# Denominator sums of cross-attention: four steps to a tile in 24 quarters of the second sequence, and one bank for the last turn

## The chip, the cores and the metric

The kernel runs on one core of one Trainium2 chip. The metric is the time on the device, in microseconds (us), of one execution. Names of engines: TensorE (PE) multiplies matrices, VectorE (DVE) and ScalarE (ACT) read and write its result banks, GpSimd (POOL) adds between tiles and issues some of the DMAs, SyncE (SP) issues the others.

## The reference, cut to what matters

A decoder layer over two sequences of 1024 tokens with 512 numbers each: a linear attention, a cross-attention to 2048 context rows, and a mixture of eight experts, each followed by a layer norm. The change lies in the cross-attention:

```python
q = (x1 @ wq.T)...; k = (x2 @ wk.T)...; v = (x2 @ wv.T)...   # 16 heads of 32
dots = jnp.einsum('bhnd,bhmd->bhnm', q, k) * SCALE
attn = jax.nn.softmax(dots, axis=-1)
out = jnp.einsum('bhnm,bhmd->bhnd', attn, v)
```

The softmax divides by the sum of exponentials over the 2048 context rows: the denominators. Numerators and denominators are summed apart, and the division comes last.

## The kernel before, in words

The attention runs in 16 **turns**. A turn takes one group of four heads of one sequence and one half (512) of its queries. Turns 0 to 7 are the first sequence, 8 to 11 the first half of the second sequence's queries, 12 to 15 the second half; 15 is LAST. A turn has 16 **steps**, one for each 128 context rows. A step has four scores (one matmul of 98x128 by 98x512 for each head, L1409), four exponentials on ScalarE (L2165) that write a tile `probs` of 128 x 4 x 512, and the numerators (L1420, eight records).

The loop goes by **blocks** of two steps, eight to a turn. The scores of the following block alternate with matmuls for the maxima (L1390) of a turn about one and a half ahead; VectorE takes each maximum (L1752, 64 to a turn, up to the fourth block of turn 14). Then come one unit of side work (rows after the attention, router), due shifts, the numerators of both steps, due divisions and inversions, and the visits for the denominators. Every engine follows the same plan in its own order; a wait stands in front of an instruction and holds all that is behind it on that engine.

**Denominators.** The two tiles of a block are added to one: GpSimd in four instructions (`add_head`, L2287) or, from the middle of turn 14, VectorE in one (`add_pair`, L1766). Four steps are a **quarter**. A *plain* quarter sends each pair's sum to TensorE; a quarter *by fours* adds its two sums into one by an accumulating DMA on GpSimd's queue (`add_four`, L2291), issued one block after the second pair. `by_fours` decides: all of turns 0 to 7 but the last quarter, and what is in LATER_FOURS. TensorE sums a tile over its partitions by eight matmul records with ones (L1442), into a bank taken from the ring `next_s_bank`; that is a **visit**, and a visit takes all tiles of a turn that are due. A pair is due one block after its addition, a quarter by fours four blocks after its second pair, or three if it is in LAST_BEFORE_PLAIN. VectorE turns the bank into `den_t` (L1773), after the visit before it has been added; GpSimd (in turn 15 VectorE: L1782, L1785) adds one column of each block of `den_t` to `den_s`. There is one `den_t` and one `den_s`. After the last visit of a turn VectorE inverts (L1793, L1794) and GpSimd divides (L2327); the first addition of a turn waits for the inversion of the turn before.

**Banks.** Eight. Bank 6 holds the numerators. Scores go round banks 0, 1, 2; maxima, shifts, side work and denominators round 4, 5, 3, 7. From the fifth block of turn 14 on there are no maxima and all share one ring of seven: 0 to 5 and 7 (SPARE). Whoever takes a bank waits until its holder before has been emptied: a denominator bank by the transpose, a score bank by the exponential.

**The end.** The last visit of turn 15 has three tiles: the sum of steps 12 and 13, and steps 14 and 15 as they are. The numerators of these two stand behind it in TensorE's order, then the inversion and division by quarters of the queries, the output rows, the router and the experts.

Lines of the excerpt: `by_fours`, `den` and `add_den` in the tables of signals, `denominators`, `add_denominators`, the loop over turns, `denominators_of`, `turn_den`, `add_den`, `invert`.

## Time and profile before

| | us |
|---|---|
| median of 3 runs | 1871.95 |
| lowest, highest | 1870.49, 1872.1 |
| the profiled execution | 1867.24 |
| its span (first to last instruction) | 1865.3 |
| attention loop, turns 0 to 15 | about 484 to 1363 of the span |
| busy: TensorE, VectorE, ScalarE, GpSimd | 1838.5, 1260.0, 878.8, 849.6 |

Busy time of TensorE is modelled from overlapping matmuls, so that a busy TensorE need not be at its peak; where it loses time is to be seen in the order of time. A turn ends where ScalarE copies its numerators out of bank 6 (L2173): turn 7 at 876.0, turn 8 at 943.8, turn 9 at 1001.3, turn 10 at 1070.2, turn 11 at 1129.4, turn 12 at 1188.5, turn 13 at 1254.6, turn 14 at 1304.5, turn 15 at 1362.9. The granted clock of TensorE is 0.997 of full speed over the span.

### The profile page before, as it was taken

To read this page: it belongs to the slowest core of one execution; us is meant where nothing else is said; L and a number is where in the kernel's file an instruction comes from. 1 tells how busy PE (TensorE), PEld (TensorE's weight loads), DVE (VectorE), ACT (ScalarE), POOL (GpSimd) and SP (SyncE) were. 2 spreads that over 40 slices of the span, in tenths; PEclk is the share of its full clock that TensorE was granted. 3 is DMA by queue.
4 is the path that set the end of the run, shared out by engine and by line. 5 is a ranking of instruction groups with operands and counts; after the bars stand their busy time and mean duration, and the time that the engine had idled before them with its cause. 6 is when DMAs were issued, how large, how long until landed. Compare 5 with 4: busy or idle time off the path is not lost.

```text
span 1865.3 us, 27888 instructions
## 1 busy us (share of the span) xinstructions
PE 1838.5 (99%) x10488; PEld 1290.2 (69%) x10488; DVE 1260.0 (68%) x2352; ACT 878.8 (47%) x1587; POOL 849.6 (46%) x822
## 2 busy tenths in 40 slices
PE   9999999999999999999999999999989999999998
PEld 8786687778655555555555554554469998899986
DVE  6675574278787888888798699778554444344457
ACT  4322323221666666666465465557624443344433
POOL 4002201000598999998677677676122223222232
PEclk9999999999999999999999999999999999999999
DMA  8003525684767686758445443451244454534544
GB/s 289 24 1 118 194 96 180 200 241 145 169 141 167 136 201 130 173 120 178 106 131 121 101 115 88 112 114 65 78 156 122 131 141 108 144 90 133 142 113 153
DMA packets 124502, 250.19 MB, mean 134 GB/s; under 512 B 11312, under 2 KB 29504, under 8 KB 119680
## 3 DMA queue, kind: packets, MB, share of 16 engines
q1 hardware_dynamic: 109696, 187.56, 34.2%
q0 software_dynamic: 14672, 60.85, 15.9%
q8 instruction: 83, 1.36, 0.3%
q14 instruction: 51, 0.42, 0.1%
HBM read 148.46 MB, written 62.42 MB: 113 GB/s over the span
## 4 chain that ended last, share of the span: by engine, by line
PE 87%; DVE 9%; DMA 2%; issue 1%; POOL 1%; ACT 0%; SPq 0%; DVEq 0%; POOLq 0%; ACTq 0%
PE banks L1221 36%; PE banks L1534 12%; PE banks L1409 11%; PE banks L1420 11%; PE banks L1390 10%; DVE max L1752 5%; PE banks L1442 4%; PE banks L1227 2%; DVE den_t L1773 1%; PE banks L1321 1%; DMA k_stack<-k_parts 0%; DMA k_half<-in_xwk_t 0%; POOL x_nat L2298 0%; DVE hot_row L1937 0%; DVE probs L1766 0%
## 5 line engine op out<-in xcount | busy, mean ns | idle before, releaser
L2287 POOL TENSOR_TENSOR probs<-probs,probs 128x512 f32<-128x512 f32 x464 | 584.4, 1304 | 192.2 <-PE banks L1420 191.4
L1752 DVE TENSOR_REDUCE max<-banks 128x1 f32<-128x512 f32 x1024 | 625.7, 678 | 37.9 <-PE banks L1390 37.5
L2165 ACT ACTIVATE probs<-banks 128x512 f32<-128x512 f32 x1024 | 517.6, 626 | 283.8 <-PE banks L1409 283.2
L1409 PE MATMUL banks<-q_stack,k_stack 98*128 98x512 f32 x1024 | 403.0, 406 | 1.1 <-DVE den_t L1773 1.0
L1390 PE MATMUL banks<-k_stack,q_stack 98*128 98x512 f32 x1024 | 399.2, 398 | 1.9 <-DVE den_t L1773 1.3
L1409 PEld LDWEIGHTS banks<-q_stack,k_stack 98*128 98x128 f32 x1024 | 190.9, 187 | 151.3 <-issue 100.6
L1420 PE MATMUL banks<-probs,v_grp 128*32 128x512 f32 x2048 | 249.7, 600 | 0.0
L1390 PEld LDWEIGHTS banks<-k_stack,q_stack 98*128 98x128 f32 x1024 | 192.4, 188 | 48.1 <-DVE max L1752 13.1
L2347 POOL DMA_INDIRECT y_rows<-eo,tok x35 | 69.8, 1994 | 173.3 <-DVE eo L1992 118.9
L1420 PEld LDWEIGHTS banks<-probs,v_grp 128*32 128x32 f32 x2048 | 60.1, 109 | 117.9 <-issue 111.6
L1979 DVE TENSOR_TENSOR hid_lo<-hid,hid_hi 128x640 fp32r<-128x640 f32 x64 | 52.7, 824 | 126.4 <-ACT hid_hi L2234 126.4
L1221 PE MATMUL banks<-w_hi,hid_hi 128*128 128x512 f32 x320 | 128.7, 402 | 0.0
L2298 POOL TENSOR_TENSOR x_nat<-x_nat,bxo_row 128x512 f32<-128x512 f32 x16 | 21.2, 1359 | 232.4 <-PE banks L1227 232.4
L1221 PE MATMUL banks<-w_hi,hid_lo 128*128 128x512 f32 x320 | 126.3, 395 | 0.0
L1221 PE MATMUL banks<-w_lo,hid_hi 128*128 128x512 f32 x320 | 125.9, 393 | 0.0
L1534 PE MATMUL banks<-xe_hi,w_hi 128*128 128x320 f32 x512 | 118.8, 309 | 0.0
L1534 PE MATMUL banks<-xe_hi,w_lo 128*128 128x320 f32 x512 | 118.7, 309 | 0.0
L1534 PE MATMUL banks<-xe_lo,w_hi 128*128 128x320 f32 x512 | 118.6, 309 | 0.0
L2229 ACT ACTIVATE hid<-banks,b1c 128x640 f32<-128x640 f32 x64 | 50.8, 793 | 139.8 <-PE banks L1534 139.8
L1773 DVE STREAM_TRANSPOSE den_t<-banks 128x512 f32<-128x512 f32 x84 | 59.9, 713 | 80.0 <-PE banks L1442 75.9
L2338 POOL DMA_INDIRECT xg<-x_rows,tok x40 | 39.1, 977 | 156.7 <-PE banks L1227 127.9
L1442 PE MATMUL banks<-probs,ones 128*32 128x512 f32 x744 | 98.1, 593 | 3.6 <-DVE probs L1766 2.0
(274 smaller groups left out, 2795.6 us busy)
## 6 DMA issues: line engine op xcount, KB each, us to landing
k_stack<-k_parts SPq DMA_DIRECT2D x144, 256.0 KB, 5.3
probs<-probs POOLq DMA_DIRECT2D x36, 1024.0 KB, 9.9
w_raw<-in_L_ffn_w SPq DMA_DIRECT2D x16, 2048.0 KB, 9.5
q_stack<-q_parts SPq DMA_DIRECT2D x48, 256.0 KB
v_grp<-v_rows SPq DMA_DIRECT2D x48, 256.0 KB, 3.6
raw<-in_ctx_t SPq DMA_DIRECT2D x8, 1024.0 KB, 6.4
k_parts<-out_hi SPq DMA_DIRECT2D x32, 256.0 KB, 2.6
k_parts<-out_lo SPq DMA_DIRECT2D x32, 256.0 KB, 3.1
```

The costliest lines, as they stand in the source:

```text
L1221: done = nc.tensor.matmul(out, lhsT, rhs, start=start and n == 0, stop=stop and n == len(operands) - 1)
L1390: nc.tensor.matmul(out, queries_of(t)[:, j, tile_of(k)], keys_of(t)[0:STK + SHIFT, j, mc * HALF:(mc + 1) * HALF], start=True, stop=True) \
L1409: nc.tensor.matmul(out, keys_of(t)[0:STK + SHIFT, j, tile_of(s)], queries_of(t)[:, j, :], start=True, stop=True).then_inc(scored.sem, 1)
L1420: done = nc.tensor.matmul(bank(NUM)[j * DH:(j + 1) * DH, :], v_grp[:, s, j * DH:(j + 1) * DH], probs_of(t, s)[:, j, :], start=s == 0, stop ...
L1442: done = nc.tensor.matmul(out[j * DH:(j + 1) * DH, :], ones[:, 0:DH], tile[:, j, :], start=n == 0, stop=n == len(tiles) - 1)
L1534: done = nc.tensor.matmul(both[:, h, 0:HC], w, x[:, h * HC:(h + 1) * HC], start=n == 0, stop=n == len(terms) - 1)
L1752: V.reduce_max(max4[:, tiles_of(t), :, :][:, k, j, mc:mc + 1], bank(bank_of["max", t, mc, k, j]), AX.X) \
L1773: V.transpose(den_t[:, :], bank(bank_of["den", t, s])).then_inc(den_turned.sem, 1)
L1979: V.tensor_tensor(hid_lo[:, f, :], hid[f % 2][:, :], hid_hi[:, f, :].bitcast(F32), ALU.subtract) \
L2165: S.activation(probs_of(t, s)[:, j, :], bank(bank_of["score", t, s, j]), ACT.Exp, scale=SCALE) \
L2287: G.tensor_tensor(a[:, j, :], a[:, j, :], b[:, j, :], ALU.add).then_inc(pair_added.sem, 1)
L2347: G.indirect_dma_start(out=y_rows, in_=eo[turn % EO][:, :], in_offset=None, compute_op=ALU.add, out_offset=bass.IndirectOffsetOnAxis(ap=to ...
```

## The change

1. LATER_FOURS, five quarters before, holds 24: all quarters of turns 8 to 13 but the last of turn 11, and the first of turn 14. (11, 2) joins (7, 2) in LAST_BEFORE_PLAIN.
2. In turn 15 all visits sum into one bank, SPARE, which is taken at the first visit. `start` is set only there and `stop` only at the last. VectorE turns the bank once, after the last visit, and takes the reciprocals from `den_t` itself; `add_den` is gone for this turn on both engines, and with it the signal last_den_added.
3. From the fifth block of turn 14 the common ring has six banks, 0 to 5, and denominators of turn 15 take none of them.

```diff
--- before.py
+++ after.py
@@ -56,9 +56,9 @@
 TILES_Y = 2
 FOUR = 4
 
-LAST_BEFORE_PLAIN = {(2 * NG - 1, 2)}
-
-LATER_FOURS = {(8, 0), (8, 1), (10, 1), (13, 0), (13, 1)}
+LAST_BEFORE_PLAIN = {(2 * NG - 1, 2), (3 * NG - 1, 2)}
+
+LATER_FOURS = {(t, q) for t in range(2 * NG, 4 * NG - 2) for q in range(4)} - {(3 * NG - 1, 3)} | {(4 * NG - 2, 0)}
 PARTS = 3
 PIECES_Y = B * NT // TILES_Y
 HALF_Y = B * NT // 2
@@ -365,7 +365,7 @@
         ones_in, xwo_in, y_in = signals("ones_in", 2, 64), signal("xwo_in", 4 * 16), signals("y_in", NH, 16)
         parts_in = signal("parts_in", 16)
         max_scored, max_taken = signal("max_scored"), signal("max_taken")
-        top_taken, inverted, den_turned, last_den_added = signals_on("tops_inverses", 4)
+        top_taken, inverted, den_turned = signals_on("tops_inverses", 3)
         top_hi, shift_copied = signals_on("shift_parts", 2)
         shift_turned = signal("shift_turned")
         scored, exp_done = signal("scored"), signal("exp_done")
@@ -453,8 +453,8 @@
             "add_pair": lambda t, s: (last_pair_added,),
             "add_head": lambda t, s, j: (pair_added,),
             "add_four": lambda t, s: (fours_added[four_of(t, s)],),
-            "den": lambda t, s: (den_summed, den_turned),
-            "add_den": lambda t, s: (last_den_added if t == LAST else den_added,),
+            "den": lambda t, s: (den_summed, den_turned) if t < LAST or s == MT - 1 else (den_summed,),
+            "add_den": lambda t, s: (den_added,),
             "copy_num_tile": lambda t, k: (num_copied,),
             "invert": lambda t, k: (inverted,),
             "divide": lambda t, k: (divided,),
@@ -852,15 +852,22 @@
                 den_steps[visit] = steps
                 den_visit.update(((t, s), visit) for s in steps)
                 den_begun.setdefault(t, visit)
-                do("den", *visit, ring=next_s_bank)
-                summed.append(visit)
+                if t < LAST:
+                    do("den", *visit, ring=next_s_bank)
+                    summed.append(visit)
+                    continue
+                if den_begun[t] == visit:
+                    take_bank(("den", t, MT - 1), SPARE)
+                do("den", *visit)
+                if steps[-1] == MT - 1:
+                    divisions.extend((t, k) for k in BY_VECTOR + BY_TENSOR)
 
         def add_denominators():
             while summed:
                 t, s = summed.pop(0)
                 do("add_den", t, s)
                 if s == MT - 1:
-                    divisions.extend((t, k) for k in (BY_VECTOR + BY_TENSOR if t == LAST else (WHOLE,)))
+                    divisions.append((t, WHOLE))
 
         do("load_consts")
         for c in range(NC):
@@ -955,7 +962,7 @@
                 following = (turn, s + 2) if s + 2 < MT else (turn + 1, 0)
                 end = turn == LAST and s == MT - 2
                 if (turn, s) == (LAST - 1, HALF_TURN):
-                    next_score_bank = next_s_bank = Ring(0, 1, 2, 3, 4, 5, SPARE)
+                    next_score_bank = next_s_bank = Ring(0, 1, 2, 3, 4, 5)
 
                 def scores(units):
                     for u in units:
@@ -988,7 +995,6 @@
                     do("rows_first", B - 1, NH - 1, BY_TENSOR[0])
                     pending.append((clock, turn, s + 1))
                     denominators(clock)
-                    add_denominators()
                 do("num", turn, s)
                 do("num", turn, s + 1)
                 if end:
@@ -1196,9 +1202,7 @@
 
         visits = [unit[1:] for unit in plan if unit[0] == "den"]
         visit_before = dict(zip(visits, (None, *visits)))
-
-        def den_added_of(t, s):
-            return (last_den_added if t == LAST else den_added)[t, s]
+        last_added = [unit[1:] for unit in plan if unit[0] == "add_den"][-1]
 
         def probs_before(t, s):
 
@@ -1423,7 +1427,9 @@
                 done.then_inc(num_summed.sem, 1)
 
             def denominators_of(t, s):
-                out = free_bank("den", t, s)
+                begun = t < LAST or den_begun[t] == (t, s)
+                visit = ("den", t, s if t < LAST else MT - 1)
+                out = free_bank(*visit) if begun else bank(bank_of[visit])
                 tiles = [probs_of(t, step - 1) for step in den_steps[t, s]]
                 if t == LAST and s == MT - 1:
                     tiles.append(probs_of(t, s))
@@ -1440,7 +1446,7 @@
                 for n, tile in enumerate(tiles):
                     for j in range(HG):
                         done = nc.tensor.matmul(out[j * DH:(j + 1) * DH, :], ones[:, 0:DH], tile[:, j, :],
-                                                start=n == 0, stop=n == len(tiles) - 1)
+                                                start=begun and n == 0, stop=n == len(tiles) - 1 and (t < LAST or s == MT - 1))
                 done.then_inc(den_summed.sem, 1)
 
             def rows_first(b, h, k):
@@ -1766,31 +1772,24 @@
                 V.tensor_tensor(a[:, :, :], a[:, :, :], b[:, :, :], ALU.add).then_inc(last_pair_added.sem, 1)
 
             def turn_den(t, s):
-                before = visit_before[t, s]
+                if t == LAST and s < MT - 1:
+                    return
                 dve.wait_ge(*den_summed[t, s])
-                if before:
-                    dve.wait_ge(*den_added_of(*before))
+                if visit_before[t, s]:
+                    dve.wait_ge(*den_added[last_added if t == LAST else visit_before[t, s]])
                 V.transpose(den_t[:, :], bank(bank_of["den", t, s])).then_inc(den_turned.sem, 1)
-
-            def add_den(t, s):
-                if t < LAST:
-                    return
-                dve.wait_ge(*den_turned[t, s])
-                rows = den_t[:, :].rearrange("p (b c) -> p b c", c=DH)[:, :, 0]
-                if den_begun[t] == (t, s):
-                    dve.wait_ge(*inverted[t - 1, WHOLE])
-                    V.tensor_copy(den_s[:, :], rows).then_inc(last_den_added.sem, 1)
-                else:
-                    dve.wait_ge(*last_den_added[visit_before[t, s]])
-                    V.tensor_tensor(den_s[:, :], den_s[:, :], rows, ALU.add).then_inc(last_den_added.sem, 1)
 
             def invert(t, k):
                 blocks = slice(0, HALF // DH) if k == WHOLE else slice(k * P // DH, (k + 1) * P // DH)
                 if k in (WHOLE, BY_VECTOR[0]):
-                    dve.wait_ge(*den_added_of(t, MT - 1))
+                    if t == LAST:
+                        dve.wait_ge(*den_turned[t, MT - 1])
+                    else:
+                        dve.wait_ge(*den_added[t, MT - 1])
                     if t:
                         dve.wait_ge(*divided[t - 1, HT - 1])
-                    step.settle(V.reciprocal(den_r[:, :], den_s[:, :]))
+                    sums = den_t[:, :].rearrange("p (b c) -> p b c", c=DH)[:, :, 0] if t == LAST else den_s[:, :]
+                    step.settle(V.reciprocal(den_r[:, :], sums))
                 V.transpose(den_c[:, :].rearrange("p (b c) -> p b c", c=DH)[:, blocks, :],
                             den_r[:, blocks].unsqueeze(2).to_broadcast([P, blocks.stop - blocks.start, DH])) \
                     .then_inc(inverted.sem, 1)
@@ -2039,7 +2038,7 @@
                     "values": values, "queries": queries, "kv": kv_sums, "mask_kv": mask_kv, "heads": heads,
                     "turn_heads": turn_heads, "project": project, "norm1": norm1, "turn_x1": turn_x1, "max": take_max, "shift_high": shift_high,
                     "xq": lambda *key: split_part("xq", *key), "ctx_k": lambda *key: split_part("ctx_k", *key),
-                    "add_pair": add_pair, "invert": invert, "den": turn_den, "add_den": add_den, "zero_counts": zero_counts, "rows": rows,
+                    "add_pair": add_pair, "invert": invert, "den": turn_den, "zero_counts": zero_counts, "rows": rows,
                     "parts": parts, "row_root": row_root, "row_shift": row_shift, "fold": fold, "fold_turn": fold_turn, "logits": logits,
                     "route_top": route_top, "route_counts": route_counts, "route_weights": route_weights,
                     "ranks": ranks, "route_slots": route_slots, "hot": hot, "table": table_sums, "tokens": tokens,
@@ -2305,8 +2304,6 @@
                     .then_inc(top_lo.sem, 1)
 
             def add_den(t, s):
-                if t == LAST:
-                    return
                 pool.wait_ge(*den_turned[t, s])
                 rows = den_t[:, :].rearrange("p (b c) -> p b c", c=DH)[:, :, 0]
                 if den_begun[t] == (t, s):
```

## Rows read from the trace of the kernel before

**Rows 1.** The page: busy time, share of the span and instructions of each engine; the chain by engine.

```profile
PE 1838.5 (99%) x10488; PEld 1290.2 (69%) x10488; DVE 1260.0 (68%) x2352; ACT 878.8 (47%) x1587; POOL 849.6 (46%) x822
...
PE 87%; DVE 9%; DMA 2%; issue 1%; POOL 1%; ACT 0%; SPq 0%; DVEq 0%; POOLq 0%; ACTq 0%
```

**Rows 2.** Turns 7 and 9: length, busy PE PEld DVE ACT POOL, clock, DMA share, GB/s.

```profile
826.50:876.00 49.50, 49.50 (x294) 28.32 (x290) 42.51 (x71) 33.12 (x68) 46.10 (x46) 1.00 0.75 166
...
943.80:1001.30 57.50, 57.15 (x346) 30.20 (x342) 53.45 (x121) 36.59 (x72) 43.43 (x46) 1.00 0.48 125
```

**Rows 3.** Order of time, a block without tile: start us, us, engine, line.

```profile
851.86 0.50 PE L1409 MATMUL banks<-q_stack,k_stack 98*128 98x512 f32 x1
...
857.57 0.50 PE L1409 MATMUL banks<-q_stack,k_stack 98*128 98x512 f32 x1
```

**Rows 4.** Order of time, a block with one tile, turn 9.

```profile
953.00 0.50 PE L1409 MATMUL banks<-q_stack,k_stack 98*128 98x512 f32 x1
...
959.59 0.50 PE L1409 MATMUL banks<-q_stack,k_stack 98*128 98x512 f32 x1
```

**Rows 5.** Line L2291, the accumulating DMA's issue (ns), and its landing (us).

```profile
L2291 POOL DMA_DIRECT2D probs<-probs x36: 825/870/945, 494.8 to 1232.6; - x36
...
DMA to landing us min/median/max: 6.9/9.9/14.3
```

**Rows 6.** Order of time, third block of turn 11, and turn 12 at 1158.88.

```profile
1085.85 0.50 PE L1409 MATMUL banks<-q_stack,k_stack 98*128 98x512 f32 x1
...
1086.46 0.24 DVE L1793 RECIPROCAL den_r<-den_s 128x16 f32<-128x16 f32 x1
...
1086.74 0.71 DVE L1794 STREAM_TRANSPOSE den_c<-den_r 128x512 f32<-128x512 f32 x1
...
1087.38 0.67 DVE L1773 STREAM_TRANSPOSE den_t<-banks 128x512 f32<-128x512 f32 x1
...
1090.90 1.07 PE L1420 MATMUL banks<-probs,v_grp 128*32 128x512 f32 x8
...
1158.88 1.06 PE L1442 MATMUL banks<-probs,ones 128*32 128x512 f32 x8 [1.53 <-DVE max L1752]
```

**Rows 7.** Order of time, turn 14: fourth and fifth block.

```profile
1284.02 5.01 POOL L2287 TENSOR_TENSOR probs<-probs,probs 128x512 f32<-128x512 f32 x4 [1.67 <-PE banks L1420]
...
1285.49 2.33 PE L1409 MATMUL banks<-q_stack,k_stack 98*128 98x512 f32 x8
...
1288.99 0.23 POOL L2318 TENSOR_TENSOR den_s<-den_s,den_t 128x16 f32<-128x16 f32 x1
...
1291.30 2.25 DVE L1766 TENSOR_TENSOR probs<-probs,probs 128x2048 f32<-128x2048 f32 x1
...
1291.46 2.18 POOL L2318 TENSOR_TENSOR den_s<-den_s,den_t 128x16 f32<-128x16 f32 x1 [2.06 <-DVE den_t L1773]
```

**Rows 8.** Order of time, turn 15, a block with a weight split.

```profile
1325.26 1.23 DVE L1969 TENSOR_TENSOR w_lo<-w_raw,w_hi 128x1024 fp32r<-128x1024 f32 x1 [2.15 <-ACT w_hi L2215]
...
1327.16 0.73 PE L1409 MATMUL banks<-q_stack,k_stack 98*128 98x512 f32 x2 [1.01 <-DVE den_t L1773]
```

**Rows 9.** Order of time, the last two blocks of turn 15.

```profile
1347.80 2.12 PE L1409 MATMUL banks<-q_stack,k_stack 98*128 98x512 f32 x8
...
1348.33 4.03 ACT L2165 ACTIVATE probs<-banks 128x512 f32<-128x512 f32 x8 [3.31 <-PE banks L1409]
...
1352.42 1.93 PE L1420 MATMUL banks<-probs,v_grp 128*32 128x512 f32 x16
...
1355.14 1.12 PE L1221 MATMUL banks<-y_nat,identity 128*128 128x512 f32 x2
...
1355.27 0.72 DVE L1773 STREAM_TRANSPOSE den_t<-banks 128x512 f32<-128x512 f32 x1 [2.05 <-PE banks L1442]
...
1355.91 2.25 DVE L1766 TENSOR_TENSOR probs<-probs,probs 128x2048 f32<-128x2048 f32 x1
...
1358.31 2.78 PE L1442 MATMUL banks<-probs,ones 128*32 128x512 f32 x24 [2.05 <-DVE probs L1766]
```

## The prediction

> **What bounds the kernel now.** I read the page first: TensorE is busy 99% of the span and holds 87% of the chain that ended last, VectorE 9%, GpSimd 1% [rows 1]. So a second on TensorE in the attention loop is worth a second of time as long as nothing else is late there. The page mixes stages, so the next view is the busy time of each engine turn by turn [rows 2]. Turn 7 (first sequence, four denominator tiles) takes 49.5 us with TensorE busy through all of it, VectorE 42.5 and GpSimd 46.1. Turn 9 (second sequence, eight denominator tiles) takes 57.5 us, and there VectorE is busy 53.4 us, 93%. The reader is to see two things: TensorE sets the pace, and in the second sequence VectorE follows close behind it. The third view is the order in time inside single blocks of two steps.
>
> **Part 1: 19 more quarters by fours.** LATER_FOURS goes from 5 quarters to 24. A quarter by fours has one tile (8 matmul records) for the denominators, a plain one has two, so 19 tiles leave TensorE. Their price: a block without a tile goes from 851.86 to 857.57, 5.71 us [rows 3]; one with a tile from 953.00 to 959.59, 6.59 us [rows 4]. The difference is 0.88 us (the tile's own record says 1.04, but it overlaps its neighbours). 19 x 0.88 = **-16.7 us**. All 19 lie in turns 8 to 14, where TensorE has no gap of its own, so they stand on the path.
>
> What it adds is 19 accumulating DMAs on GpSimd's queue at 0.87 us of GpSimd each [rows 5], against fewer denominator additions of 0.23 us. In turn 9 that makes 43.4 + 4 x 0.87 - 4 x 0.23 = 46.0 us of GpSimd in about 53 us; turn 7 carries 46.1 in 49.5 without holding TensorE [rows 2], so I take 0. Landing takes 6.9 to 14.3 us [rows 5], and the visit comes three blocks behind the issue, 17.1 us at 5.71 each: 0. The one quarter that is visited a block earlier, (11, 2), has 11.4 us plus its place in the block; turn 7 has the same pattern. Without cover it would cost up to 14.3 - 11.4 = 3 us once. So 0, bounds 0 and +3.
>
> **Part 2: VectorE's queue in turns 8 to 14.** The visits fall from 46 to 29 there, each with a 0.72 us transpose: 12.2 us less of VectorE against 16.7 less of TensorE, so its share stays about where it is. What changes is the place. In plain turns the inversion of the turn before and a transpose land together in the third block: [rows 6] show 0.71 + 0.67 us (and a reciprocal of 0.24) ahead of the maxima, and scores and maxima take 1085.85 to 1090.90, 5.05 us where 3.9 is usual. Four turns have such a block, 4.0 us together. By fours, the inversion moves to the fifth block, which has no transpose. Once TensorE also waits 1.53 us for a bank for a tile that goes [rows 6]. In all I count 15 blocks from turn 9 on with 11 us of such waiting. Against this a block without a tile gives VectorE less room: 0.88 us shorter for 0.72 us less work. I take **-3 us**, nearest to the four blocks; bounds -8 (nearly all goes) and +3 (15 blocks x 0.16, rounded up).
>
> **Part 3: two visits in one block.** The last quarter of turn 13 is now due three blocks into turn 14, and so is the plain pair (14, 5). No other block gets visits of two turns, and before there was none. Both use the one den_t: VectorE's second transpose waits until GpSimd has added the first, and in GpSimd's queue that addition stands behind the four additions of the pair (14, 7). [Rows 7]: those four start at 1284.02 and the addition follows at 1288.99; the next block's scores start at 1285.49, or 1286.4 with one tile more ahead of them. So the second transpose runs from about 1289.4 to 1290.1. The ring (4, 5, 3, 7) has by then given 928 banks to maxima, 14 to shifts, 25 to the fold and the rows' units and 54 to visits; 1021 leaves 1 by four, so its bank is number 5, which the sixth score of the next block takes from the new ring of six, due at 1286.4 + 1.3 = 1287.7. TensorE waits 2.5 us. Behind it on VectorE stand 3.3 us of routing weights, the inversion (0.95) and the transpose of (14, 7), which ends just after the next sixth score wants its bank: 0.2 more. **+2.7 us**; bounds 0 (bank not wanted) and +6 (VectorE stays behind through the turn).
>
> Here a rule of the Trainium skill bears. The row first: beside VectorE's pair addition (two inputs in SBUF) GpSimd's addition takes 2.18 us instead of 0.23 [rows 7]. The page "SBUF — State Buffer" (Who interferes with whom) says that a VectorE instruction with two SBUF inputs contends with a GpSimd one that reads SBUF; by that rule, which this row bears out, each denominator addition in the rest of turn 14 is late by 2 us, and the sum would be +4.7 here instead of +2.7. The same page says that descriptor writing on GpSimd can be starved by a VectorE copy in a two-port mode; the issues of 0.83 to 0.95 us [rows 5] show nothing of it.
>
> **Part 4: the last turn.** The nine tiles stay; six of seven transposes go, and so do the seven small additions on VectorE. VectorE has gaps there, so only places count where TensorE waited on them. First: the seventh score of one block waited 1.01 us for the bank of a tile whose transpose stood behind a weight split [rows 8]. That bank is no longer in the ring: **-1.0 us**. Second, the end: the transpose of (15, 11) starts at 1355.27, the last pair addition only behind it at 1355.91, and the last three tiles wait 2.05 us for that addition [rows 9]. The addition needs the numerators of step 12, which begin at 1352.42 and are through half of 1.93 later, about 1353.4; a row addition is off VectorE by then too. Without the transpose it runs to 1355.7, before the identity matmuls (from 1355.14, 1.12 us) end. The wait goes: **-2.1 us**. The split of w1 that follows comes earlier by as much and is late for nothing. The direct reading of den_t saves 0.4 us on VectorE beside ScalarE's copies: 0.
>
> Against this the ring has six banks instead of seven from the middle of turn 14. The eighth score now needs the second exponential instead of the first. In [rows 9] scores start at 1347.80, exponentials at 1348.33 with 0.50 each, so the second is out at 1349.34, while the eighth weight load is due at about 1349.3. About 0.07 x 12 blocks = **+0.8 us**; bounds 0 and +4 (0.35 in each block, if ScalarE is behind).
>
> **Sum.** -16.7 - 3 + 2.7 - 1.0 - 2.1 + 0.8 = -19.3 us. The profiled execution took 1867.24 us (span 1865.3 and 1.9 around it): 1847.9. The median of the runs is 4.7 above it, so I forecast 1871.95 - 19.3 = 1852.7, say 1853.
>
> **Rivals.**
> (a) VectorE holds the turns of the second sequence. For it: 93% busy in turn 9, and TensorE is already late by 11 us. Against it: VectorE is relieved as much as TensorE. The waits then grow by 3 instead of shrinking by 3, and part 3 costs 6: -16.7 + 3 + 6 - 1.0 - 2.1 + 0.8 = -10.0, 1862.
> (b) VectorE's waits nearly vanish: -8 in place of -3 and part 3 at 0: -27, 1845. For it: blocks of the first sequence show no waits at all. Against it: routing work, which makes the lumps, stays.
> (c) Slower: the accumulating DMAs of the second sequence land late, because weights, rows and key parts share the 16 engines. The place is the first tile of each visit, where TensorE waits for fours_added. Up to 17.1 us it costs nothing; at 18.1 us 19 waits of 1 us eat the whole gain, from there on it is slower, and at 20 us it is 19 x 2.9 - 19.3 = +36, 1908. Against it: turn 7 moves more in less time (DMA share 0.75 against 0.48 in turn 9 [rows 2]) and TensorE never waits.
> (d) The room lies in TensorE's own blocks: its records fill the time, but in turn 9 and its like it waits between them, and the removed tiles fill with waiting. If the 11 tiles of turns 9, 11 and 12 brought nothing, the sum would be -19.3 + 11 x 0.88 = -9.6, 1862. For it: turn 9 is 8.0 us longer than turn 7, and four tiles are only 3.5 of it. Against it: the block of [rows 4] stands in turn 9 and has no such waiting. The Trainium skill's page "Perfetto Trace Analysis" (Identifying the Most-Contended Engine) says that matmul busy time tells little of how near TensorE is to its limit and that weight-load time is the better sign. By that rule, with weight loads at 28.3 of 49.5 us in turn 7 and 30.2 of 57.5 in turn 9 [rows 2], turn 9 has the more room, as (d) says.
> (e) The change does nothing: a denominator tile hidden elsewhere. [Rows 3, 4] exclude it, each block by the next one's start.
>
> **How the numbers follow.** Forecast (-13 to -24) 0.70; (a) and (d) together 0.14; (b) 0.07; (c) 0.05; a gain lost to several waits, between -9 and 0, 0.04. The range 1845 to 1863 takes in (a), (b) and (d) and leaves out about 0.1 to 0.15. A measurement of this kernel tells about 0.2%, 3.7 us: faster 0.93, within it 0.02, slower 0.05.
>
> **What would show it.** 592 records of the denominator matmul instead of 744, 61 transposes instead of 84, 55 accumulating DMAs instead of 36. Turn 9 near 53 us, turn 11 near 55, turn 14 about 52 (part 3 more, one tile fewer). In turn 14 a wait for the transpose of (14, 5) in the middle of the fifth block's scores; no wait of 2.05 us ahead of the last tiles. Landing above 17 us, or TensorE waiting for a DMA at a tile, would make the forecast wrong; so would waits for maxima in turns 9 to 12 that sum to more than 14 us.

## The result, and the profile after

The changed kernel is slower by about 1%: a median of 1888.89 us (4 runs, 1885.32 to 1889.22) against 1871.22 us (4 runs, 1868.97 to 1872.1), ratio 1.0097 with the interval [1.0084, 1.011]. I had forecast 1853. The profiled execution took 1885.32 us, its span is 1883.5 us (1865.3 before). Single executions that took over 10% longer than the rest (two of e3_own_block, a few of the kernel before) are left out of every median and ratio below.

The page of the changed kernel: busy time and instructions, the chain by engine, the matmuls for the maxima (L1394) and for the scores (L1413).

```profile
PE 1839.5 (98%) x10336; PEld 1293.8 (69%) x10336; DVE 1265.7 (67%) x2322; ACT 882.0 (47%) x1587; POOL 863.6 (46%) x824
...
PE 86%; DVE 10%; DMA 1%; issue 1%; POOL 1%; ACT 0%; SPq 0%; DVEq 0%; POOLq 0%; ACTq 0%
...
L1394 PE MATMUL banks<-k_stack,q_stack 98*128 98x512 f32 x1024 | 405.8, 404 | 18.9 <-DVE max L1758 18.5
L1413 PE MATMUL banks<-q_stack,k_stack 98*128 98x512 f32 x1024 | 408.7, 412 | 3.5 <-DVE den_t L1780 2.3
```

Against [rows 1], 152 matmuls are gone as planned (19 tiles x 8), yet TensorE's busy time is 1.0 us higher and not 17 lower. The third row is the find: TensorE stood 18.5 us before matmuls for the maxima, because VectorE had not taken the maxima before them and no bank was free. In the kernel before, the same line (L1390 there) waited 1.3 us between 480 and 1400 us, all of it for a bank with denominators and none for a maximum.

The engines by turn, for turns 9 to 15 (length, busy PE PEld DVE ACT POOL, clock, DMA share, GB/s):

```profile
943.90:1006.30 62.40, 56.41 (x310) 30.89 (x310) 58.82 (x120) 37.11 (x72) 46.12 (x46) 0.95 0.83 200
1006.30:1073.60 67.30, 67.15 (x343) 35.59 (x338) 50.82 (x89) 33.69 (x67) 46.49 (x46) 1.00 0.68 157
1073.60:1137.10 63.50, 56.34 (x314) 30.63 (x310) 58.17 (x111) 37.61 (x72) 45.92 (x46) 0.95 0.77 179
1137.10:1200.40 63.30, 59.31 (x319) 32.98 (x314) 51.31 (x94) 34.50 (x67) 45.32 (x44) 0.92 0.56 126
1200.40:1273.00 72.60, 67.72 (x334) 35.98 (x330) 57.35 (x97) 33.71 (x68) 46.04 (x46) 0.95 0.65 138
1273.00:1326.50 53.50, 50.76 (x310) 24.69 (x302) 40.04 (x90) 35.84 (x72) 35.18 (x34) 0.97 0.38 99
1326.50:1381.30 54.80, 53.41 (x315) 22.48 (x308) 31.27 (x32) 32.53 (x62) 7.97 (x6) 1.00 0.19 68
sum 437.40, PE 411.09 PEld 213.25 DVE 347.77 ACT 244.99 POOL 273.05; mean PE 58.73 PEld 30.46 DVE 49.68 ACT 35.00 POOL 39.01
```

The same stretches of the kernel before:

```profile
sum 419.10, PE 410.60 PEld 210.45 DVE 342.12 ACT 242.06 POOL 260.80; mean PE 58.66 PEld 30.06 DVE 48.87 ACT 34.58 POOL 37.26
```

| turn | 8 | 9 | 10 | 11 | 12 | 13 | 14 | 15 |
|---|---|---|---|---|---|---|---|---|
| before, us | 67.8 | 57.5 | 68.8 | 59.3 | 59.1 | 66.1 | 49.9 | 58.4 |
| after, us | 66.5 | 62.3 | 67.3 | 63.6 | 63.3 | 72.5 | 53.5 | 54.8 |

Turns 8 and 10 gained 1.3 and 1.5 us, where two and three missing tiles should give 1.8 and 2.6, the last turn gained 3.6, and turns 9, 11, 12, 13 and 14 lost 3.6 to 6.4 each. The two sums account for it. In turns 9 to 15 TensorE is idle 437.4 - 411.1 = 26.3 us, before 8.5: **+17.8 us**. Its busy time should have fallen by the 17 tiles of these turns, 17 x 0.88 = 15.0 us, and rose by 0.5: **+15.5 us**. This is a remainder; I put it down to matmuls that ran longer at a lower clock. The granted clock, 0.92 to 0.97 in the losing turns and 1.00 in turns 10 and 15, gives nearly the same: each turn's length times the share of the clock that is missing makes about 17 us over these turns, and 2 before. 17.8 + 15.5 - 15.0 = +18.3 us over these turns.

Where one such loss comes from, in order of time, turn 9 (start us, us, engine, line, [idle before, what ended it]):

```profile
990.65 0.87 POOL L2324 TENSOR_TENSOR heads_t<-num_c,den_c 128x128 f32<-128x128 f32 x2
...
991.47 0.90 POOL L2290 DMA_DIRECT2D probs<-probs  x1
...
992.10 0.17 DVE L1927 CAST slot_i<-slot 128x8 int32<-128x8 f32 x1
...
992.12 5.18 POOL L2286 TENSOR_TENSOR probs<-probs,probs 128x512 f32<-128x512 f32 x4
992.31 5.03 DVE L1928 TENSOR_SCALAR slot_row<-slot_i 128x8 int32<-128x8 int32 x1
992.72 0.19 PEld L1413 LDWEIGHTS banks<-q_stack,k_stack 98*128 98x128 f32 x1 [0.84 <-issue]
...
997.25 0.16 DVE L1929 TENSOR_SCALAR slot_col<-slot_i 128x8 int32<-128x8 int32 x1
...
998.27 0.80 PE L1394 MATMUL banks<-k_stack,q_stack 98*128 98x512 f32 x1 [5.05 <-DVE max L1758]
...
998.86 0.63 PE L1413 MATMUL banks<-q_stack,k_stack 98*128 98x512 f32 x1
```

The reader is to see three steps. GpSimd issues the accumulating DMA and begins its four additions directly behind it. A VectorE operation on 8 columns, whose twin one line further takes 0.16 us, takes 5.03 us and ends when the last addition does. Behind it stand the maxima, so TensorE has no bank for 5.05 us; after that wait its matmuls take 0.63 us instead of 0.39 to 0.40 for the next eleven. The same picture stands at 1123.42 (5.10 us, then 4.89 of TensorE's waiting) and 1259.31 (5.10, then 4.84). Elsewhere a small VectorE operation is held for one addition, about 1.2 us. Turn 12 has no long hold, but three of 1.27 to 1.55 us one behind the other (1163.39 to 1167.96), a wait of 2.30 us behind them, and the lowest clock of all, 0.92.

What sets the three long holds apart is in the trace too. Of the 24 accumulating DMAs from turn 8 on, exactly three (issued at 991.47, 1122.68 and 1258.60) have the additions directly behind them: GpSimd had come late from the divisions that stand just ahead, and the first addition's record begins 0.20 to 0.24 us before the issue's record ends. Behind the other 21 GpSimd's next operation begins at least 0.13 us after the issue's record. These three are the three long holds. The second of them:

```profile
1122.68 0.86 POOL L2290 DMA_DIRECT2D probs<-probs  x1
1123.31 5.18 POOL L2286 TENSOR_TENSOR probs<-probs,probs 128x512 f32<-128x512 f32 x4
```

```profile
1123.42 5.10 DVE L1898 TENSOR_TENSOR before<-before,rt_ms 128x8 f32<-128x8 f32 x1
```

I call the excess of VectorE's SBUF operations over the shortest of the same line and shape, where it is over 0.6 us, **held time**; it is taken from the one profiled execution of each kernel. Between 480 and 1400 us it is 7.9 us in the kernel before and 26.8 us after.

The double visit of turn 14 came as forecast, 2.28 us where I had 2.5:

```profile
1300.08 4.97 POOL L2286 TENSOR_TENSOR probs<-probs,probs 128x512 f32<-128x512 f32 x4 [1.78 <-PE banks L1424]
...
1305.01 0.23 POOL L2315 TENSOR_TENSOR den_s<-den_s,den_t 128x16 f32<-128x16 f32 x1
1305.34 0.72 DVE L1780 STREAM_TRANSPOSE den_t<-banks 128x512 f32<-128x512 f32 x1 [2.94 <-POOL den_s L2315]
...
1306.11 0.96 PE L1413 MATMUL banks<-q_stack,k_stack 98*128 98x512 f32 x3 [2.28 <-DVE den_t L1780]
```

And the last tiles of turn 15 wait for nothing, where [rows 9] had 2.05 us:

```profile
1375.69 1.12 PE L1225 MATMUL banks<-y_nat,identity 128*128 128x512 f32 x2
1376.74 2.78 PE L1448 MATMUL banks<-probs,ones 128*32 128x512 f32 x24
```

The accumulating DMAs, issue (ns) and landing (us), to be read beside [rows 5]:

```profile
L2290 POOL DMA_DIRECT2D probs<-probs x55: 787/870/940, 496.0 to 1291.3; - x55
...
DMA to landing us min/median/max: 6.9/10.7/14.2
```

### The profile page after: what moved, and what is told of

Its sections match the earlier page's. It is cut to its first block, busy times and chain, and to the rows that moved or that the text cites. A ratio compares the mean times of both kernels' runs of the same rounds, so it can differ in the third digit from the quotient of the medians.

```text
span 1883.5 us, 27511 instructions
## 1 busy us (share of the span) xinstructions
PE 1839.5 (98%) x10336; PEld 1293.8 (69%) x10336; DVE 1265.7 (67%) x2322; ACT 882.0 (47%) x1587; POOL 863.6 (46%) x824
## 4 chain that ended last, share of the span: by engine, by line
PE 86%; DVE 10%; DMA 1%; issue 1%; POOL 1%; ACT 0%; SPq 0%; DVEq 0%; POOLq 0%; ACTq 0%
PE banks L1225 36%; PE banks L1540 12%; PE banks L1413 11%; PE banks L1424 11%; PE banks L1394 10%; DVE max L1758 5%; PE banks L1448 3%; PE banks L1231 2%; PE banks L1325 1%; DVE den_t L1780 0%; DMA k_half<-in_xwk_t 0%; DVE rsqrt_y L1715 0%; POOL x_nat L2297 0%; DVE before L1898 0%; DVE slot_row L1928 0%
## 5 line engine op out<-in xcount | busy, mean ns | idle before, releaser
L1394 PE MATMUL banks<-k_stack,q_stack 98*128 98x512 f32 x1024 | 405.8, 404 | 18.9 <-DVE max L1758 18.5
L1413 PE MATMUL banks<-q_stack,k_stack 98*128 98x512 f32 x1024 | 408.7, 412 | 3.5 <-DVE den_t L1780 2.3
L1413 PEld LDWEIGHTS banks<-q_stack,k_stack 98*128 98x128 f32 x1024 | 194.1, 191 | 156.3 <-issue 102.6
L1394 PEld LDWEIGHTS banks<-k_stack,q_stack 98*128 98x128 f32 x1024 | 195.6, 191 | 69.9 <-DVE max L1758 35.8
L1988 DVE TENSOR_TENSOR eo<-banks,b2s 128x512 f32<-128x512 f32 x35 | 24.2, 692 | 106.1 <-PE banks L1225 106.1
L1780 DVE STREAM_TRANSPOSE den_t<-banks 128x512 f32<-128x512 f32 x61 | 43.7, 716 | 73.7 <-PE banks L1448 68.7
```

The costliest lines, as they stand in the source:

```text
L1394: nc.tensor.matmul(out, queries_of(t)[:, j, tile_of(k)], keys_of(t)[0:STK + SHIFT, j, mc * HALF:(mc + 1) * HALF], start=True, stop=True) \
L1413: nc.tensor.matmul(out, keys_of(t)[0:STK + SHIFT, j, tile_of(s)], queries_of(t)[:, j, :], start=True, stop=True).then_inc(scored.sem, 1)
```

## The experiments

Theory 1, made once the two traces had been laid side by side: GpSimd's additions, above all directly behind the issue of a DMA, hold VectorE's small SBUF operations, and TensorE waits for maxima. Theory 2: something else in the change does it (the DMA traffic, the shorter blocks, the new last turn). Edits are against the changed kernel, unless another is named.

### The two halves apart

e1_fours_only keeps the sums of four and has the last turn as before. e2_last_only keeps the last turn and has:

```diff
-LAST_BEFORE_PLAIN = {(2 * NG - 1, 2), (3 * NG - 1, 2)}
...
-LATER_FOURS = {(t, q) for t in range(2 * NG, 4 * NG - 2) for q in range(4)} - {(3 * NG - 1, 3)} | {(4 * NG - 2, 0)}
+LAST_BEFORE_PLAIN = {(2 * NG - 1, 2)}
...
+LATER_FOURS = {(8, 0), (8, 1), (10, 1), (13, 0), (13, 1)}
```

> The fours of the second sequence alone; the last turn sums, turns and adds as before. Theory (the four stretches of turns 9 to 13 in which a small VectorE operation is held for 5 us and TensorE's clock falls behind it carry the loss): nearly the whole loss stands here, 20 to 23 us over the kernel before, since the last turn gave 3.6 us back. Rival (the loss comes from the ring of six banks or the bank held through the last turn): near the kernel before less 16 us.

> The one bank and the ring of six alone, with the five quarters by fours of before. Theory: 3 to 4 us faster than before, as turn 15 was (58.3 to 54.8 us in the two traces). Rival (turn 15 only gained because turn 14 lost and its work had piled up before it): within 1 us of before.

e1: 1883.51 us, ratio 1.0063 [1.0039, 1.0087], single runs from 1874 to 1895. e2: 1866.98 us, ratio 0.9976 [0.9964, 0.9989]. The loss is in the sums of four; the last turn is worth about 4 us by itself. e1's held time is 27.0 us, e2's 7.9. Two things don't fit. I had expected e1 at 20 to 23 us over the kernel before, and its median is 13 over. And the halves don't add up: +0.63% and -0.24% against +0.97% for both together. e1's ten runs spread over 21 us, and their granted clock with them, from 0.994 in the two fastest to 0.985 in the slowest; 0.009 of 1890 us is 17 us, so nearly all of the spread is TensorE's clock.

### Moving the DMA

e3_own_block issues each accumulating DMA at the end of its own pair's block (first sequence too) instead of the next one; e7_behind, in the second sequence and without the quarter (11, 2), puts it behind the next pair's additions:

```diff
                 if not end:
-                    while fours:
-                        do("add_four", *fours.pop())
...
                     elif s % FOUR == 2:
-                        fours.append((turn, s + 1))
+                        do("add_four", turn, s + 1)
```

```diff
...
                             do("add_head", turn, s + 1, j)
+                    while behind:
+                        do("add_four", *behind.pop())
```

> The changed kernel, but each accumulating DMA is issued in the block of its own second pair, right behind that pair's four additions, and not a block later just ahead of the next pair's. Theory (four additions that start directly behind the issue hold a VectorE operation for all four): between the issue and the next four additions stand a wait for numerators or the divisions, so no hold of 5 us is left, the clock stays up, and the time is 1850 to 1858. Rival (19 more transfers of 1 MB, or VectorE's lost room, carry the loss): it stays within 5 us of the changed kernel, 1884 to 1890.

> The changed kernel, but in turns 8 to 14 (without (11, 2)) the accumulating DMA is issued behind the next pair's four additions instead of ahead of them. Theory: the next additions then wait for numerators first, and the gap lets VectorE in, as long as GpSimd is not late; it is early in the second sequence except where divisions stand there. So holds of 5 us vanish, and the time is 1853 to 1862. Rival (any issue within some microseconds ahead of additions holds): it stays above 1875. The visits then have two blocks and the end of a third behind the issue; if TensorE waits for landings there, it shows at the denominator tiles.

e3: 1877.7 us (ten runs from 1870.3 to 1879.6), ratio 1.0031 [1.0017, 1.0045]; e7: 1891.57 us, ratio 1.0117 [1.0096, 1.0138]. Both times miss what theory 1 promised. e3 still has two long holds, in turns 9 and 12. In one of them two divisions fill the place between DMA and additions:

```profile
1149.39 0.88 POOL L2288 DMA_DIRECT2D probs<-probs  x1 [0.30 <-POOL probs L2284]
1149.99 1.35 POOL L2322 TENSOR_TENSOR heads_t<-num_c,den_c 128x128 f32<-128x128 f32 x2
1151.11 5.10 POOL L2284 TENSOR_TENSOR probs<-probs,probs 128x512 f32<-128x512 f32 x4
1156.00 1.02 POOL L2322 TENSOR_TENSOR heads_t<-num_c,den_c 128x128 f32<-128x128 f32 x2
```

```profile
1151.08 6.13 DVE L1938 TENSOR_TENSOR hot_col<-hot_col,weight 128x160 f32<-128x160 f32 x1
```

This hold ends at 1157.21 us. The last addition ends at 1156.21; what ends at 1157.02 is a second pair of divisions directly behind it. So it lasted until GpSimd's whole run without a gap was over, divisions included.

Turn by turn e3 speaks for theory 1. Turns 11 and 13 have no long hold in it and take 57.8 and 66.1 us at full clock, 63.6 and 72.5 in the changed kernel; turns 9 and 12, with the long holds, take 62.9 and 62.1. What e3 gains there it loses in part in turns 14 and 15, 56.6 and 58.0 us at a clock of 0.94.

In e7 one long hold is left, at 1122.09 us, and it stands directly behind the one issue of turn 11 that the edit leaves ahead of the additions, that of (11, 2). But in turn 13 five small operations in a row are held, begun between 1254.74 and 1260.47 us, one for 2.06 us and four for 1.2 us each, and TensorE waits 4.8 us for the maxima behind them. Held time is 22.2 us in e3 and 24.3 in e7. So the long holds go where the place of the DMA says, but they are not all of it: a row of single holds costs as much as a long one, and a place for the DMA alone doesn't mend it.

### The hold by itself

e4_probe and e5_probe2 leave the whole computation out: VectorE does small additions (128x8) one behind the other, while GpSimd issues a DMA and does four 128x512 additions, each phase three times.

```diff
+G.dma_start(c[:, :, :], d[:, :, :], accum_op=ALU.add).then_inc(landed, 16)
+for j in range(4):
+    G.tensor_tensor(a[:, j, :], a[:, j, :], b[:, j, :], ALU.add).then_inc(done, 1)
```

> No attention at all: a kernel that only measures and returns copies of a part of x. VectorE runs 36 operations of 128x8 with two inputs in SBUF in a row, while GpSimd runs one of ten patterns, three times each. Theory: without a DMA and with the DMA's landing awaited, a VectorE operation that meets the four additions is held for one addition at a time, about 1.3 us; with the accumulating DMA issued directly ahead, one operation is held for about 5 us, with two additions behind it about 2.5 us; with a wait between issue and additions, at most 1.3. Rival (it is the length of the queue of additions): the same 5 us without a DMA. Rival (the transfer itself, not the issue, holds VectorE): 5 us with no additions at all, and none with the DMA of 128x8. Open: whether a plain DMA and operations with one input do the same.

> The measuring kernel again (no attention), with 64 operations in a row on VectorE so that they outlast everything. Theory (after a DMA issue on GpSimd, a run of additions with no gap keeps VectorE out of SBUF until the run ends, and a gap in the run lets it in): together 5.7 us as before; with the additions begun only after VectorE's 11th, 15th, 21st or 31st operation, holds of 1.2 us for each addition once the gap is long enough, and the shortest such gap is what I want to see; each addition waiting for the one before: several holds of about 1.3 us and none over 2; the second alone waiting: one of 1.3 and one of about 3.7; the DMA between the second and the third addition: two of 1.2, then one of 2.5 to 3; landed before: holds of 1.2 at most. Maxima out of a bank of PSUM: no hold at all, with the DMA or without. Rival (whatever the gap, four additions after an issue hold it for all four until the transfer has landed): 5 us in all of the gaps below 7 us.

VectorE's additions in e4, first the phase without a DMA, then the one with it (x how many: ns min/median/max, first and last start):

```profile
L60 DVE TENSOR_TENSOR small_w<-small_u,small_v x36: 152/154/1232, 21.0 to 28.0; 128x8 f32<-128x8 f32 x36
```

```profile
L60 DVE TENSOR_TENSOR small_w<-small_u,small_v x16: 153/154/5670, 44.8 to 51.4; 128x8 f32<-128x8 f32 x16
```

Without a DMA an operation of 0.154 us is held for 1.23 us, once for each addition of GpSimd. Behind a DMA one operation is held for 5.67 us, from 44.76 us, 0.43 us before the first addition's record begins, to the end of the fourth (50.40). What does and doesn't matter:

| phase | longest VectorE operation, us |
|---|---|
| no DMA, four additions | 1.23 |
| accumulating DMA | 5.65 to 5.85 |
| plain DMA; a small addition between | 5.4; 5.65 |
| DMA of 128x8; VectorE with one input | 5.7; 5.7 |
| the additions begin once VectorE's 12th operation is done (e4) | 5.3 to 5.5 |
| two additions instead of four | 3.2 to 3.3 |
| DMA without additions | 0.16 |
| first addition 0.25 us after the issue record's end, or later | 1.23 |
| each addition waits for the one before | 2.05, then 1.25 |
| only the second addition waits for the first | 2.03, then 1.23 to 1.25 |
| DMA between second and third addition | 1.23, 1.23, 3.25 |
| VectorE reduces a PSUM bank instead | 0.69 (not held) |

Two rows of e5: the additions directly behind the issue, then with a gap of 0.25 us.

```profile
L66 DVE TENSOR_TENSOR small_w<-small_u,small_v x20: 152/157/5132, 98.5 to 105.0; 128x8 f32<-128x8 f32 x20
```

```profile
L66 DVE TENSOR_TENSOR small_w<-small_u,small_v x15: 153/155/1234, 119.1 to 124.5; 128x8 f32<-128x8 f32 x15
```

A row without any DMA is that of the bank's reduction beside four additions, 0.68 us as in the kernel's maxima. The phases that were to begin after the DMA's landing told nothing, since VectorE's operations were over by then. With only the second addition waiting I had expected one hold of 1.3 us and one of 3.7; it came otherwise, and one pause is enough to end the long hold for all that follows. So the hold is real, was seen on operations with SBUF operands and not on the reduction of a PSUM bank, and is multiplied by a DMA issue directly ahead.

### Cutting the run

e6_each_waits makes each addition of the second sequence wait for the one before:

```diff
                 pool.wait_ge(*num_summed[t, s - 1])
+                if t >= B * NG and j:
+                    pool.wait_ge(*pair_added[t, s, j - 1])
```

> The changed kernel, but from turn 8 on each of GpSimd's four additions of a pair waits for the one before it. Theory: no hold of VectorE over 1.6 us is left, only the double visit's 2.3 us and its clock; with part of the added waits on GpSimd (96 x about 0.1 us, hidden) the time is 1853 to 1860. Rival (the four additions and their length hold TensorE anyway, or GpSimd gets too slow): no faster than the changed kernel, 1880 and above.

1884.19 us, ratio 1.0063 [1.0045, 1.008]: missed. No hold exceeds 2.09 us, yet the held time is 22.9 us, now in twenty pieces, and TensorE waits 14.0 us for maxima in eight places (longest 3.2) and 4.2 at two tiles. The profiled execution is the slowest of the six, 1892.01 us. The number of held operations matters as much as the length of the longest.

### Taking the additions' length away

e8_short_after and e9_short_before cut GpSimd's additions of the second sequence in the two kernels to 32 of 512 columns. All instructions, transfers and waits stay; the other 480 columns of these sums are left out.

```diff
-                G.tensor_tensor(a[:, j, :], a[:, j, :], b[:, j, :], ALU.add).then_inc(pair_added.sem, 1)
+                n = DH if t >= B * NG else HALF
+                G.tensor_tensor(a[:, j, 0:n], a[:, j, 0:n], b[:, j, 0:n], ALU.add).then_inc(pair_added.sem, 1)
```

> The changed kernel with GpSimd's additions of the second sequence cut to the first 32 of the 512 columns of each half tile (it leaves out the rest of those sums; every instruction, DMA, wait and TensorE block stays in its place and number). In e9_short_before the kernel before is cut in the same way. Theory 1, that the loss is VectorE's small operations held beside GpSimd's additions: a cut addition is over in a fraction of 1.25 us, so no operation of VectorE is held for 5 us and few for 1, and what is left is TensorE's gain by 19 tiles of 0.88 us; the time comes to 1845 to 1855 us and lies 14 to 20 us below that of e9. Theory 2, that the transfers, the blocks' own order on TensorE or VectorE's room make the loss: none of these is touched, and the time stays at 1875 us or more, not below that of e9.

> The kernel before with the same cut of GpSimd's additions in the second sequence (32 of 512 columns; the rest of those sums is left out). It is the control of e8_short_after. Theory 1: before has 7.9 us of held operations of VectorE from 480 to 1400 us against 26.8 after, and most of them fall where TensorE doesn't wait for them, so the cut gives 0 to 6 us: 1865 to 1871 us. Theory 2: the cut changes nothing, 1870 to 1872 us.

e8: 1847.8 us (1846.58 to 1849.11), ratio to the kernel before 0.9887 [0.9872, 0.9901]. e9: 1865.3 us, ratio 0.9973 [0.9963, 0.9983]. With short additions the change is worth -17.5 us where it costs +17.7 with long ones. Both have no held time. The block of turn 9 that lost 5 us, in e8:

```profile
987.32 0.88 POOL L2291 DMA_DIRECT2D probs<-probs  x1
...
989.51 0.17 DVE L1927 CAST slot_i<-slot 128x8 int32<-128x8 f32 x1
989.72 0.17 DVE L1928 TENSOR_SCALAR slot_row<-slot_i 128x8 int32<-128x8 int32 x1
```

TensorE's waits from 850 to 1363 us in e8, and in the changed kernel (us in total, times, longest):

```profile
PE banks L1413 <- ACT probs L2164: 1.3, 3, 1.0
PE banks L1394 <- DVE max L1758: 1.1, 2, 0.6
```

```profile
PE banks L1394 <- DVE max L1758: 18.5, 7, 5.0
PE banks L1413 <- DVE den_t L1780: 2.3, 1, 2.3
```

Turns 9 and 11 of e8 take 53.6 and 53.6 us. The transfers, the blocks and VectorE's instructions are those of the changed kernel, so theory 2 is out as a cause by itself: none of these costs anything without the long additions. Turn 14 takes 48.4 us and has no wait for `den_t`: the double visit also costs only what GpSimd's additions make it cost. One thing e8 can't part: it also gives GpSimd's own queue room.

### The DMAs' share

e10_no_dma leaves the accumulating DMAs of the second sequence out (the second pair's sum isn't added to the first; the tile waits for GpSimd's last addition). The additions stay.

```diff
-                        do("add_four", *fours.pop())
+                        job = fours.pop()
+                        if job[0] < B * NG:
+                            do("add_four", *job)
```

> The changed kernel without the accumulating DMAs of the second sequence (the sum of the second pair of each quarter isn't added onto the first, so the denominators there hold one pair of two; the matmuls on the fours' tiles wait for GpSimd's last addition instead of the DMA). GpSimd's additions stay. Theory 1, held operations: without the DMA ahead of them four additions hold an operation of VectorE for one addition (1.23 us) and not for all (5.1 us), so the four TensorE waits of about 5 us for maxima with the fallen clock behind them go, while the single holds stay: 1860 to 1875 us, and no hold above 2 us. Theory 2, that the blocks without a tile leave VectorE too little room whatever GpSimd does: 1880 us or more.

1869.83 us, ratio 1.0 [0.9986, 1.0013], held time 13.3 us, no hold over 1.42 (both as expected); TensorE waits 5.3 us for maxima in seven places (longest 1.0). That is 19 us below the changed kernel and 22 above e8: about a half of what the long additions cost goes away with the DMAs, and the single holds and GpSimd's queue are left for the other. e10 takes out the issues, 0.87 us of GpSimd for each of 24, and the transfers together; that the issue is enough to make the long hold is shown by e4, where a DMA of 128x8 does it too.

### Where it pays

e11_chosen has the new last turn and sums of four where the short blocks hold few of VectorE's small operations, and none in turn 14:

```diff
-LAST_BEFORE_PLAIN = {(2 * NG - 1, 2), (3 * NG - 1, 2)}
...
-LATER_FOURS = {(t, q) for t in range(2 * NG, 4 * NG - 2) for q in range(4)} - {(3 * NG - 1, 3)} | {(4 * NG - 2, 0)}
+LAST_BEFORE_PLAIN = {(2 * NG - 1, 2), (10, 2)}
...
+LATER_FOURS = {(8, 0), (8, 1), (10, 0), (10, 1), (10, 2), (12, 2), (12, 3), (13, 0), (13, 1)}
```

> The changed last turn, with sums of four steps in nine quarters of the later turns: (8,0), (8,1), (10,0), (10,1), (10,2), (12,2), (12,3), (13,0), (13,1), and sums of pairs everywhere else there; they are quarters whose tile-less blocks hold none or few of VectorE's small operations, and turn 14 has none, so that its double visit goes. Theory 1 (held operations make the loss, and a tile saved where none is held is worth 0.88 us): e2_last_only's 1867 us less four more tiles than the kernel before saves: 1861 to 1865 us, below both kernels. Theory 2 (a tile-less block costs about what it saves, wherever it stands): 1866 to 1872 us.

1864.41 us (1861.89 to 1866.24), ratio 0.9973 [0.9961, 0.9985]: faster than the kernel before by 0.3%, and than the changed one by 1.3%. Turns 10 and 12 gained 2.6 and 1.7 us on the kernel before, turn 11 lost 0.9, for which I have no cause. Held time is 7.9 us as before. Two of its nine issues (1024.6 and 1180.6 us) have the additions directly behind them; no small VectorE operation falls there, and none is held. Against e2 (0.9976) the four tiles are not told apart by the intervals; the medians differ by 2.6 us and the spans by 1.7. Turns 8 to 14 of the two traces, where the tiles lie, differ by 3.2 us, near to 4 x 0.88 = 3.5.

Held time and median time side by side, kernels with the tiles of the changed kernel (592 denominator matmuls): e8 0 and 1847.8; e10 13.3 and 1869.8; e3 22.2 and 1877.7; e6 22.9 and 1884.2; e7 24.3 and 1891.6; the changed kernel 26.8 and 1888.9; e1, which lacks the new last turn, 27.0 and 1883.5. With 744: e9 0 and 1865.3; before 7.9 and 1870.2 in the same runs. The order is nearly kept. From e8 to the changed kernel 26.8 us held go with 41.1 us of time, about one and a half for one; the lower clock behind the waits and GpSimd's own queue are both in it.

The same by turn, from the profiled executions (length, held time in us, granted clock):

| turn | before | changed | e3 | e10 | e8 |
|---|---|---|---|---|---|
| 9 | 57.5, 1.0, 1.00 | 62.3, 7.4, 0.95 | 62.9, 7.2, 0.95 | 59.6, 2.9, 0.94 | 53.6, 0, 1.00 |
| 11 | 59.3, 2.0, 1.00 | 63.6, 9.8, 0.95 | 57.8, 4.1, 1.00 | 59.1, 5.9, 1.00 | 53.6, 0, 1.00 |
| 12 | 59.1, 1.7, 1.00 | 63.3, 2.9, 0.92 | 62.1, 6.6, 0.95 | 58.5, 1.1, 0.94 | 55.5, 0, 1.00 |
| 13 | 66.1, 0, 1.00 | 72.5, 5.7, 0.95 | 66.1, 1.8, 1.00 | 67.4, 1.8, 1.00 | 65.3, 0, 1.00 |

In every turn with a long hold the clock falls, and turns 9, 11 and 12 then take 62 us or more. Without one the clock may fall or not: 2.9 us held in single pieces go with 0.92, 5.9 us with 1.00.

## Why the prediction was wrong

**What held.** The counts: 592 denominator matmuls, 61 transposes, 55 accumulating DMAs. The size of the gain, where nothing is held: e8 against e9 gives -17.5 us for all four parts, forecast -19.3. By turn it is 13.3 us in turns 8 to 14, 0.70 us for each of the 19 tiles where I had 0.88, and 3.5 in turn 15. The landing stayed under 14.3 us and TensorE waited for no DMA, so rival (c) fell. The double visit: 2.28 us for 2.5. GpSimd's busy time in turn 9: 46.1 us for 46.0.

**Part 1 is the step that failed.** It took the 19 issues as 0.87 us of a GpSimd that has time to spare, by the comparison of turn 7, which "carries 46.1 in 49.5 without holding TensorE". That row was read rightly and says nothing of turn 9: turn 7 has 71 VectorE instructions, nearly all maxima that read PSUM and are not held; turn 9 has 121, and the fifty more are router and row operations on SBUF. The price is not paid in GpSimd's time but in VectorE's, through the access they share. Two causes meet. A block without a tile is shorter by 0.88 us, and a block with an issue holds 0.87 us more of GpSimd's time beside 5.0 us of additions, so that less of GpSimd's idle time is left in which the small operations pass freely; single holds rise from 8 to 13, and that this is the reason was argued and not tested. And additions that follow an issue directly hold one operation for all four; that is shown, by the three issues of the changed kernel, by e4 and e5 and by e3's turns 11 and 13. Measured: held time 26.8 us instead of 7.9, TensorE's waits for maxima (at the matmuls for them) 18.5 us instead of 0, and 15.5 us more in matmuls at a fallen clock; 19 tiles x 0.88 could not pay that.

**Part 2 failed with it.** "-3, bounds -8 and +3" counted instructions and their usual durations. VectorE's busy time should have fallen by 12 us and rose by 5.7 on the page. The sign that I had named, waits for maxima of more than 14 us in turns 9 to 12, came, if only just: 13.6 us at the matmuls for the maxima and 1.4 at a tile, 15.0 together, and 4.8 more in turn 13; three waits of about 5 us make 14.8 of it. What it lacked was a price beside it and more than the 5 in 100 that I left to the slow side. Rival (a) had the right engine for the wrong reason: VectorE isn't short of time, it is stopped, and it had +3 us for its waits, where idle time and the clock made +33 with the double visit in them. The 11 us of waiting in 15 blocks that the -3 started from were counted from the length of blocks; as idle time of TensorE the trace of the kernel before has 3.7 us in turns 9 to 14, and e8, with nothing held, has 3.4.

**The rule was at hand and used one way only.** I applied contention to GpSimd, whose 0.23 us addition takes 2.18 us beside VectorE's pair addition [rows 7]. The Trainium skill's page "SBUF — State Buffer" (Who interferes with whom) says that, where the two contend, whoever issues first has the shared ports for its whole instruction and the other stops. The trace agrees in the other direction too: 1.23 us for an operation of 0.15. By that rule each hold would end with one addition; the rows of 5.03 and 5.10 us, and the 5.7 us of e4, each over a run of four, go beyond what it says. My sentence that issues of 0.83 to 0.95 us "show nothing" of such a conflict looked at the issue's length; the victim was VectorE behind it. The kernel before already had holds: eight operations between 951 and 1288 us took 1.15 to 1.45 us, 7.9 us too long together.

**Part 3** had the wait right, and missed that the clock can fall behind it: the numerators after it took 3.28 us for 16 instead of 1.92, 1.4 us more. In e10 the same wait of 2.3 us left the clock of turn 14 at 1.00. The other price, +4.7, did not come: four of GpSimd's denominator additions take 2.19 us each in the rest of turn 14 and the first block of turn 15, and TensorE waits for none of them. **Part 4** was small and too cautious: -2.3 forecast, -3.6 by the turn's length, e2 -4.5 by the ratio. Part of this is the clock and not the banks: turn 15 has 0.97 in the kernel before, 1.00 in the changed one, and only 0.94 in e2's profile, where it took 57.9 us, hardly less than before. The wait of 2.05 us went as worked out; of the 0.8 us for the smaller ring nothing shows: eight scores take 2.18 to 2.21 us in turn 15, against 2.12 in [rows 9].

**Open.** Why an issue ahead stretches the hold over all the additions, and why it begins 0.43 us before the first of them, the runs don't say. Why both halves together lose more than e1's and e2's changes added up is not known either. How much of e8's gain is GpSimd's own room isn't parted from the holds. e1 spreads over 21 us from run to run, the kernel before over some 7; that small shifts of the two engines against each other decide which operation is caught fits this, and was not tested.

## What to carry to other kernels

When work is added to GpSimd, look at what VectorE has in SBUF at the same time, not at GpSimd's busy share: short operations of VectorE stand still for a whole GpSimd operation, and maxima or other work queued behind them carries the delay to TensorE. Look for an operation that takes several times its twin's time and ends with another engine's. Put a GpSimd DMA issue where a gap of 0.25 us or PSUM work of VectorE follows, and look for the issues that GpSimd comes to late, since they have no gap behind them, and price a TensorE wait of some microseconds with the slow matmuls behind it.

## What the runs showed of the hardware

- A VectorE operation on SBUF (0.15 us) beside a 128x512 addition of GpSimd: 1.23 us. A reduction of a PSUM bank: 0.68 us in either case.
- The same behind a DMA issued on GpSimd with additions directly after: 5.1 to 5.9 us for four, 3.2 to 3.3 us for two, whether the DMA adds, copies, or moves 128x8 only, and whether the VectorE operation has one input or two. With 0.25 us between the issue record's end and the first addition, or with a pause before the second, the hold is over one addition at a time: 1.23 us each.
- In each of the three waits of about 5 us TensorE's granted clock fell to the lower of its two levels (1.2 and 2.4 GHz): behind the first it is 0.50 of full speed from 998.3 to 1003.2 us, and eleven 98x512 matmuls in a row, from 998.86 to 1003.12, took 0.63 us instead of 0.39 and began every 0.43 us instead of every 0.23. Over turns 9 to 15 that took nearly as much as the waits themselves, 15.5 against 17.8 us.
